# TensorE's weighing of a head's values moved from behind the fourth score to between the second and the third

## The reference, cut to what matters

```python
scores = jnp.einsum('bihd,bjhd->bhij', q, k) / jnp.sqrt(jnp.float32(D_K))
scores = scores + jnp.transpose(bias, (2, 0, 1))[None]
attn = jax.nn.softmax(scores, axis=-1)
out = jnp.einsum('bhij,bjhd->bihd', attn, v).reshape(B, S, D)
return out @ W_out + b_out
```

## Time and profile before

| what | value |
|---|---|
| runs | 1426.77, 1421.06, 1420.52 us, median 1421.06 |
| span of the profiled execution | 1426.5 us |
| time of the profiled execution | the page gives none beside the span; the nearest of the runs is 1426.77 |
| PE busy | 1151.9 us (81% of the span) |
| PEld busy | 901.6 us (63%) |
| DVE busy | 953.5 us (67%) |
| ACT busy | 689.4 us (48%) |
| POOL busy | 582.7 us (41%) |
| mean granted clock | 0.897 |

### The profile page before, as it was taken

The page is one execution under the profiler, slowest core; times in us unless marked ns, Lnnn a source line. Parts: engine busy times, 40 slices in busy tenths (PEclk is TensorE's granted clock), DMA queues, the critical chain, the costliest instruction groups (busy, mean ns, idle before and its releaser), DMA issues. The chain is left out here.

```text
span 1426.5 us, 33135 instructions
## 1 busy us (share of the span) xinstructions
PE 1151.9 (81%) x11298; PEld 901.6 (63%) x11299; DVE 953.5 (67%) x2201; ACT 689.4 (48%) x1052; POOL 582.7 (41%) x629
## 2 busy tenths in 40 slices
PE   5469998898998988989998833699999999999000
PEld 3246776666766766667676621588888888888000
DVE  4548788686885886867889548445555455554497
ACT  4248776665766766657686501122222222222243
POOL 3216063440542434405423016444444444444596
PEclk9779999898998998989999855799999999999555
DMA  9596652666355635663552148112213212311362
GB/s 309 177 226 158 145 142 92 128 129 121 128 121 124 134 96 133 120 121 127 122 101 101 46 154 259 45 47 103 107 47 110 103 47 104 107 48 47 93 224 81
DMA packets 120463, 172.03 MB, mean 121 GB/s; under 512 B 10600, under 2 KB 95080, under 8 KB 120336
## 3 DMA queue, kind: packets, MB, share of 16 engines
q1 hardware_dynamic: 110160, 140.44, 38.1%
q0 software_dynamic: 10176, 29.90, 6.4%
HBM read 113.56 MB, written 56.74 MB: 119 GB/s over the span
## 5 line engine op out<-in xcount | busy, mean ns | idle before, releaser
L653 ACT ACTIVATE b_pr<-b_sn,b_mn 128x512 f32<-128x512 f32 x512 | 340.9, 714 | 133.3 <-DVE b_mn L731 129.4
L731 DVE CUSTOM_DVE_ANT_0 b_sn<-b_ps_s,s_tile 128x512 f32<-128x512 f32 x512 | 332.3, 685 | 90.9 <-PE b_ps_s L857 36.6
L866 PE MATMUL b_ps_t<-b_ident,b_pr 128*128 128x128 f32 x2048 | 280.0, 282 | 8.5 <-ACT b_pr L653 7.4
L866 PEld LDWEIGHTS b_ps_t<-b_ident,b_pr 128*128 128x128 f32 x2048 | 245.6, 145 | 54.2 <-ACT b_pr L653 21.0
L857 PE MATMUL b_ps_s<-b_ks,b_qs 96*128 96x512 bf16 x512 | 195.9, 405 | 57.8 <-DVE b_mn L731 30.6
L1453 PE MATMUL d_ps_u<-d_xp,k_wu 128*128 128x256 bf16 x1776 | 201.1, 273 | 0.0
L1468 PE MATMUL d_ps_y<-k_wd,d_gp 128*128 128x256 bf16 x1776 | 199.9, 273 | 0.0
L739 DVE COPY b_pt<-b_ps_t 128x1024 f32<-128x1024 f32 x128 | 156.4, 1222 | 55.0 <-PE b_ps_t L866 51.1
L1453 PEld LDWEIGHTS d_ps_u<-d_xp,k_wu 128*128 128x128 bf16 x1776 | 173.2, 98 | 21.3
L1468 PEld LDWEIGHTS d_ps_y<-k_wd,d_gp 128*128 128x128 bf16 x1776 | 173.7, 98 | 20.2
L660 ACT ACTIVATE b_pt<-b_ps_t 128x1024 f32<-128x1024 f32 x128 | 131.2, 1025 | 108.1 <-PE b_ps_t L866 107.5
(11 more groups left out here) (190 smaller groups left out, 1275.2 us busy)
## 6 DMA issues: line engine op xcount, KB each, us to landing
w_parts<-b_w_split SPq DMA_DIRECT2D x32, 512.0 KB, 3.4
splits<-b_parts SPq DMA_DIRECT2D x32, 384.0 KB, 2.6
b_qs<-splits SPq DMA_DIRECT2D x96, 128.0 KB, 5.0
b_ks<-splits SPq DMA_DIRECT2D x96, 128.0 KB, 7.1
b_w_raw<-in_w_up_t SPq DMA_DIRECT2D x16, 512.0 KB, 9.5
b_w_raw<-in_w_down_t SPq DMA_DIRECT2D x16, 512.0 KB, 5.7
k_wu<-w_parts SPq DMA_DIRECT2D x8, 1024.0 KB, 5.0
k_wd<-w_parts SPq DMA_DIRECT2D x8, 1024.0 KB, 7.8
```

The lines of the kernel that those rows point to most:

```text
L653: act.activation(pr[:, m, t, :], sn[:, t, :], ACT.Exp, bias=mn[:, m, t:t + 1], scale=-1.0).then_inc(exped, 1)
L731: dve.tensor_tensor_reduce(sn[:, t, :], ps_s[:, t % 2, :], ahead.tile[:, n, at:at + S], -1.0, BIG, ALU.add, ALU.min, mn[:, n % 2, t:t + 1] ...
L866: mm = pe.transpose(ps_t[:, j, t * P:(t + 1) * P], pr[:, m, t, j * P:(j + 1) * P], ident[:, :])
```

## The change

The call of `weigh` moves from behind score 3 to between score 1 and the shared job of head n. Which head is weighed, and with what, stays as it was. No instruction is added or removed, and no other engine's queue changes.

```diff
                     score(b, n, 0)
                     score(b, n, 1)
+                    if n > 1:
+                        weigh(b, n - 2)
+                    elif kind != "first":
+                        weigh(b - 1, n + NH - 2)
                     shared(b, n, kind)
                     if kind != "first" or n > 0:
...
                     score(b, n, 3)
-                    if n > 1:
-                        weigh(b, n - 2)
-                    elif kind != "first":
-                        weigh(b - 1, n + NH - 2)
                     shared(b, n + 0.5, kind)
```

## The result

The changed kernel took 1572.8 us (median of 4 runs, 1571.59 to 1578.14) against 1420.9 before: **1.106 times the time, 95% interval 1.103 to 1.109**, or 151.9 us more. The forecast was 1549.7 in a range of 1525 to 1591.

The account below looks back on a forecast made before the run. Attention was taken as bound by TensorE's order of work and the ring through DVE and ACT. Six middle batches (100.0), first (+12.8), last (+13.4) and seams (+2.4) gave +128.6 us, so 1549.7; range 1525 to 1591.

Parts of the forecast that it names:

- the clock: Rival: granted clock falls behind the 31 waits for ACT's copy, +27 to +53 us, about 1590; chance 0.12.
- the anchor: Whole kernel: the predicted difference in the profiled execution (span 1426.5 us) is added to the median, 5.4 us below it.
- What is removed and added: Each head: score 1 still starts at 3.57 us; weigh follows 0.31 later for 1.03, turn at 4.91 plus shared job.
- The copy's wait: Heads with n - 2 a multiple of four: weigh waits for ACT's copy of `ps_o`, starting 1.07 us later.
- The terms of a batch: Middle batch, heads 0 to 15: changes by groups of heads, 16.67 us a batch, 100.0 for six.
- the step about the order: Heads 11 and 12: DVE's centring fixes head 11's evacuation; only weigh before the projection of values is exposed, +1.03 us.
- the rival's sign: Attention: granted clock showing 0.50 behind heads 2, 6, 10 or 14 would make the clock's rival right.
- the 128.6 of the sum: Whole kernel: predicted increase in us from the middle batches, first and last batch and seams.
- No change: Rival: in attention, waiting takes up the shift as TensorE's work is the same and its queue full, 1421 us; chance 0.05.
- the copy costs nothing: Rival: at the 31 copy waits, weigh is held up elsewhere as long, 33 us less, 1517; chance 0.06.
- Faster: Rival: DVE is the bound and gains at the loop's turn and in heads 3, 6, 8; 14 us, 1407; chance 0.02.

Follow-up runs that it names:

- the experiment with halves: Against the kernel before, half of weigh (16 of 32 matmuls) moved behind score 1, the other half left behind score 3: 1511.3 us, ratio 1.063.
- the filled kernel: Changed kernel with score 3 written three times in every head and score 1 four times in heads 2, 6, 10 and 14: 1557.8 us, ratio 1.097.
- the second execution: The changed kernel measured once more, unaltered, on the chip of the filled kernels: 1573.4 us, ratio 1.109 to before.
- the run: Changed kernel with ACT's copy of `ps_o` moved from behind its fourth exp to behind its second: 1524.4 us, ratio 1.072 to before.

## Why the prediction was right, and where it was short

The direction and the mechanism were right, and the forecast was 23 us short of 151.9: 16 in attention, nearly all of it the clock, and 7 in the anchor.

*What is removed and added.* Score 1 starts at 3.57 us as said, in spite of the free queue ahead of it. Weigh starts 0.32 behind it (0.31 said) and a head with a turning job is 5.40 (5.46 said). TensorE now stands still 0.61 and 0.22 us for DVE's minima in each head, where weigh used to run, and the experiment with halves shows that the loss goes by weigh's length. One reading was wrong without harm: that in head 2 TensorE's queue was the bound, as it was busy 5.56 of 5.56 us. The stretch without a weigh took 5.56 us as well. Its length is score 1's wait and what stands behind it, and weigh filled time that was there anyway.

*The copy's wait.* 31 waits, 31.1 us in all (31 x 1.07 = 33 said), weigh at 4.95 in head 2 as said. Moving the copy took away 1.06 us per head. This term stands by a run.

*The terms of a batch.* Head 2: 7.78 (7.74 said); head 6: 7.79 (7.70); head 10: 7.79 (7.74); heads 3 to 5: 16.19 (16.38); 7 to 9: 19.29 (18.76); 13 to 15: 18.63 (18.85). These make 77.5 in sum, 77.2 said. Heads 7 to 9 have the largest error at full clock, 0.5 us a batch too little; its cause is open. The first batch's heads 3 to 15 took 76.3 (75.7 said). The last batch's heads 1 to 15 grew by 15.2 (94.19 against 78.95; 13.4 said), with three falls of the clock behind copies among them. Heads 0 and 1 took 2.2 more than before in the batch shown, rather than 0.5, but over the five turns of the loop it is 0.9 each (101.0 against 96.6 us).

*Heads 11 and 12.* I had "only weigh before the projection of values is exposed, +1.03", so 14.6 us. The batch shown took 16.83, the longest of six; the six took 94.7 us, or 15.8 each. In one of them the clock held:

```profile
245.43:259.71 14.28, 10.63 (x117) 7.77 (x116) 11.27 (x24) 7.95 (x11) 9.04 (x8) 1.00 0.28 103
```

In the filled kernel, too, the two take 14.4 at full clock. So the step about the order was right, and what it left out is a fall in five batches: TensorE waits for DVE in head 11 and again in head 12 (1.09 and 1.49 us), where weigh no longer fills the second wait, and then runs weigh and the projection at half clock.

*The clock: the term that I had put at nothing.* I made it a rival, 31 falls behind the copy's waits or none. It came in between. Of the 31 us by which half clock in attention rose (70 to 101), six falls of 3.4 us behind a copy's wait make 20: in head 2 of batches 1 and 2, in head 14 of batch 1, and in heads 2, 6 and 10 of the last, counting batches from 0. That was the rival's sign, 0.50 behind heads 2, 6, 10 or 14, in six of 31 places; the second execution had it in eight. Head 12 of the middle batches makes 10 more. At 0.47 a us the 31 are 14 to 15 us, and with the 128.6 of the sum that makes 143 of the 144.8 by which the stretch of attention grew (715.8 to 860.6). The filled kernel shows that it is the clock: 15 us less with more work. The Trainium skill ("TensorE: Matmul & The Clock Gate", Part 4) says that full clock doesn't engage for transposes, from which I had drawn that every head could fall. The trace doesn't agree: heads 3 to 5 of the changed kernel, with 8 transposes in 1.04 us, stand at 1.00.

*The anchor.* The prediction set the span of the profiled execution, 1426.5 us, against the median of times. A span is shorter than the time of its own execution, 1571.1 against 1572.79 us in the changed kernel, whose profile so lies at its median. With the same 1.7 us the profiled execution of before was at about 1428 us, an estimate, and 7 above its median. It was a long one for its kernel, so the medians grew by 7 us more than the spans.

*The rivals.* No change fell because score 1 can't start early. That the copy costs nothing fell by the run. Faster fell with them: DVE's gain at the loop's turn didn't show as time, heads 0 and 1 being 4.4 us longer over five turns. That the forecast came near isn't luck at full clock, where nearly every term holds. That it stayed within its range is owed to the clock's 15 us being small; no term of it gave them.

## What to carry to other kernels

Ask of each job in an in-order queue which wait it covers, and not only how long it is: 1.0 us of weighing lay under two biases of DVE, and moved behind the last result that this wait is for, it cost 0.4 us in a head without a shared job, where TensorE had waited for ACT's exps before, 0.8 in one with a turning job and 1.2 in one with a projection (4.52 to 4.96, 4.60 to 5.40 and 5.57 to 6.73 us). In 31 heads it met a wait that had been hidden before. Where a job is moved ahead, look also for the semaphore that was always ready in its old place. Short waits of TensorE can cost twice, through the granted clock, so compare the mean clock of the stretch before an order is judged.

## What had not been expected of the hardware

- The granted clock fell to half behind waits of no more than 1.5 us each, where several came close together (0.61, 0.22 and 0.98 us in head 2 of the changed kernel, 1.09 and 1.49 in heads 11 and 12). The same waits in head 2 left it at full in four of six middle batches, so their length alone doesn't say whether it falls. Rows of before had shown a fall only behind a wait of over 2 us or at the loop's turn.
- Redundant matmuls in those waits kept the clock up, and made a kernel with 352 (respectively 416) matmuls more faster by 15 and 60 us.
- A us at half clock cost 0.44 to 0.48 us in this kernel, nearly the full half, though much of attention is spent waiting for DVE.
